# One set of 98-column products per tile in the layers' edge stage, with the values held in on-chip memory

## The reference

```python
for i in range(L):                       # L = 4
    Q = _ln(h @ Wq[i], gq[i], bq[i])
    K = _ln(h @ Wk[i], gk[i], bk[i])
    qi = Q[src]
    kj = K[dst]
    score = (qi * kj).sum(-1) + 0.1 * (edge_attr * qi[:, :RBF]).sum(-1) + logm[dst]
    smax = jax.ops.segment_max(score, src, num_segments=N)
    es = jnp.exp(jnp.minimum(score - smax[src], 20.0))
    denom = jax.ops.segment_sum(es, src, num_segments=N)
    alpha = es / (denom[src] + 1e-10)
    m = h[dst] @ Wm[i]
    aggi = jax.ops.segment_sum(alpha[:, None] * m, src, num_segments=N)
    ...
```

## Time and profile before

| | us |
|---|---|
| median of three runs | 5786.9 (5772.91 to 5797.48) |
| the profiled execution | 5777.9 |
| its span | 5776.3 |
| TensorE busy in it | 4309.7 (75%) |
| VectorE busy | 3791.9 (66%) |
| GpSimd busy | 2681.4 (46%) |
| ScalarE busy | 2250.1 (39%) |

### The profile page before, as it was taken

One profiled execution on the slowest core, in us unless ns is written; L12 is line 12 of the kernel. 1 busy time (PEld: TensorE's weight loads), 2 busy tenths in 40 slices (PEclk: granted clock), 3 DMA queues, 4 the chain that ended last, 5 costly groups with the idle time before them and its releaser, 6 DMA issues. The chain is left out here.

```text
span 5776.3 us, 186815 instructions
## 1 busy us (share of the span) xinstructions
PE 4309.7 (75%) x79576; PEld 3592.7 (62%) x79576; DVE 3791.9 (66%) x7925; ACT 2250.1 (39%) x7746; POOL 2681.4 (46%) x2702
## 2 busy tenths in 40 slices
PE   7999994046666499759976997599757845877887
PEld 4555552035555388748874887488735733877786
DVE  6888875079998588657765785687576446545244
ACT  3333331046666255435543554355401424101310
POOL 2777777756666177517751775277520510000000
PEclk7666665569998699869987998799877977988897
DMA  9322223167775344234423442344255434000000
GB/s 352 74 73 74 70 68 74 42 150 197 195 201 166 113 161 165 92 109 167 154 92 120 157 154 92 123 154 165 80 88 196 158 106 134 2 9 4 4 4 10
DMA packets 488184, 656.80 MB, mean 114 GB/s; under 512 B 316480, under 2 KB 370372, under 8 KB 484117
## 3 DMA queue, kind: packets, MB, share of 16 engines
q1 hardware_dynamic: 450965, 595.00, 32.7%
q0 software_dynamic: 33856, 48.44, 3.4%
q10 hardware_dynamic: 2496, 0.98, 0.1%
HBM read 464.16 MB, written 180.09 MB: 112 GB/s over the span
## 5 line engine op out<-in xcount | busy, mean ns | idle before, releaser
L299 POOL DMA_INDIRECT edges<-sb_bk_rec,sb_bk_pos x782 | 784.8, 1004 | 323.7 <-issue 234.0
L1688 ACT ACTIVATE sb_at_val<-banks,sb_at_prob 128x49 f32<-128x49 f32 x3800 | 776.0, 326 | 189.7 <-PE banks L1622 183.3
L1727 DVE TENSOR_REDUCE sb_at_tops<-banks 128x1 f32<-128x512 f32 x1000 | 652.5, 661 | 279.1 <-PE banks L1602 276.7
L1578 PE MATMUL banks<-sb_near,sb_at_hotT_d 128*128 128x49 bf16 x11100 | 610.3, 184 | 74.0 <-DVE sb_at_key L1709 44.5
L1536 POOL TENSOR_TENSOR sb_at_key<-sb_at_key,sb_at_attr 128x400 f32<-128x400 f32 (+1 forms) x400 | 371.8, 930 | 581.1 <-ACT sb_at_key L1672 489.9
L1580 PE MATMUL banks<-sb_queryp,sb_at_hotT_s 128*128 128x49 bf16 x11400 | 624.5, 185 | 12.8 <-issue 12.3
L1578 PEld LDWEIGHTS banks<-sb_near,sb_at_hotT_d 128*128 128x128 fp8e4 x11100 | 560.3, 96 | 79.1 <-issue 69.3
L1580 PEld LDWEIGHTS banks<-sb_queryp,sb_at_hotT_s 128*128 128x128 fp8e4 x11400 | 559.5, 96 | 15.7 <-issue 15.7
L1543 POOL TENSOR_TENSOR sb_at_val<-sb_at_val 128x490 f32<-128x490 f32 (+1 forms) x400 | 387.4, 968 | 68.9 <-ACT sb_at_val L1688 67.4
L1672 ACT COPY sb_at_key<-banks 128x490 f32<-128x490 f32 (+1 forms) x400 | 225.3, 563 | 462.9 <-PE banks L1580 460.6
L1545 POOL TENSOR_TENSOR sb_at_val<-sb_at_val 128x490 f32<-128x490 f32 (+1 forms) x400 | 386.6, 966 | 31.4
(11 more groups left out here) (692 smaller groups left out, 10166.0 us busy)
## 6 DMA issues: line engine op xcount, KB each, us to landing
sb_at_attr<-attr SPq DMA_DIRECT2D x100, 760.0 KB, 7.5
sb_at_hotT_s<-rows_src_t SPq DMA_DIRECT2D x100, 608.0 KB, 3.9
sb_at_hot_s<-rows_src SPq DMA_DIRECT2D x100, 608.0 KB, 8.6
sb_at_hotT_d<-rows_dst_t SPq DMA_DIRECT2D x100, 592.0 KB, 5.9
edges<-sb_pad SPq DMA_DIRECT2D x95, 460.0 KB, 7.0
sb_gt_rec<-edges SPq DMA_DIRECT2D x25, 1748.0 KB
sb_we_hotT<-rows_dst_t SPq DMA_DIRECT2D x52, 592.0 KB, 5.8
attr<-sb_gt_rec SPq DMA_DIRECT2D x25, 760.0 KB, 13.2
```

What stands on the lines that cost most here:

```text
L299: pool.indirect_dma_start(list1, bass.IndirectOffsetOnAxis(pos[:, t:t + 1], 0), rec[:, k, j, :], None).then_inc(sent[k], 16)
L1578: pe.matmul(ps[:, 0, H1 * j:H1 * j + H1], where, what, start=(n == 0), stop=(n == 2))
L1688: ins = act.mul(val[:, v % VB, j, 0, :], ps[:, 5, H1 * j:H1 * j + H1], prob[:, i % 2, k:k + 1])
L1727: dve.tensor_reduce(tops[:, i % 2, g:g + 1], ps[:, 3 + x % 2, 0:P * len(RG[g])], AX, ALU.max).then_inc(s_top, 1)
```

## The change

- The two sets of three 49-column products per tile, for keys (L1578) and values (L1622), become one set of three with 98 columns (`pair`, in the keys' place). A unit's result now fills half of bank 0 and half of bank 1, five tiles each.
- The query products stand apart (`ask`), in the place of `values`, in banks 2 and 5.
- ScalarE copies keys (`key`) and then values (`held`, twelve buffers) out of the banks. `pair` waits for both copies of the unit before.
- `weigh` reads `held` and stands one slot earlier; so do `remainders` and `total` (unit u − 12 instead of u − 13). The drain is one slot shorter.
- The units have 10, 10, 10 and 8 tiles instead of 10, 10, 9 and 9. `hotT_d` has two buffers, loaded after the pairs of the block two before.
- VectorE's order stays as it was, `add` included.

```diff
-    TAKE = [range(0, 10), range(10, 20), range(20, 29), range(29, KT)]
+    TAKE = [range(0, 10), range(10, 20), range(20, 30), range(30, KT)]
...
-    VB = 4
+    VB, HB = 4, 12
+    ASK = 2, 5
...
+    held = m.sb("at_held", [P, HB, 10, H1])
...
             def first(i):
                 if i >= 4:
-
-                    sp.wait_ge(s_h, Q * (i - 3))
+                    sp.wait_ge(s_mgot, i - 3)
                 sp.dma_start(flat(hotT_s, i % 4), lists["hotT_s"][i]).then_inc(s_hotT[i % 4], 16)
-                sp.dma_start(flat(hotT_d, i % 4), lists["hotT_d"][i]).then_inc(s_hotT[i % 4], 16)
+                if i >= 2:
+                    sp.wait_ge(s_pair, Q * (i - 1))
+                sp.dma_start(flat(hotT_d, i % 2), lists["hotT_d"][i]).then_inc(s_wins[i % 2], 16)
...
-            for u in range(U + LAG + 2):
+            for u in range(U + LAG + 1):
                 i, q = divmod(u, Q)
-                if 0 <= u - LAG - 2 < U:
-                    remainders(u - LAG - 2)
+                if 0 <= u - LAG - 1 < U:
+                    remainders(u - LAG - 1)
...
-            def keys(i, q):
+            def pair(i, q):
                 u = Q * i + q
...
                 if u:
                     pe.wait_ge(s_rowk, u)
-                if u >= 2:
-                    pe.wait_ge(s_dot, u - 1)
+                    pe.wait_ge(s_held, u)
+                half = len(TAKE[q]) // 2
                 for j, k in enumerate(TAKE[q]):
                     if k == NW:
                         pe.wait_ge(s_far[i % 4], 16 * (i // 4 + 1))
                     for n in range(3):
-                        where, what = place(i, k, n, 0)
-                        pe.matmul(ps[:, 0, H1 * j:H1 * j + H1], where, what, start=(n == 0), stop=(n == 2))
+                        where, what = ((hotT_d[:, i % 2, k, :], near[:, k, n, :]) if k < NW else
+                                       (c["identb"][:], far[:, i % 4, n, :]))
+                        ins = pe.matmul(ps[:, j // half, KH * (j % half):KH * (j % half) + KH], where, what, start=(n == 0),
+                                        stop=(n == 2))
+                ins.then_inc(s_pair, 1)
+
+            def ask(i, q):
+                u = Q * i + q
...
+                if u >= 2:
+                    pe.wait_ge(s_dot, u - 1)
...
-            for u in range(U + LAG + 3):
+            for u in range(U + LAG + 2):
...
-                    keys(i, q)
+                    pair(i, q)
...
-                if 0 <= u - LAG < U:
-                    values(*divmod(u - LAG, Q))
+                if i < NB:
+                    ask(i, q)
                 if laid:
                     lay(b, laid[1])
-                if 0 <= u - LAG - 3:
-                    total(*divmod(u - LAG - 3, Q))
+                if 0 <= u - LAG - 2:
+                    total(*divmod(u - LAG - 2, Q))
...
-            def key_in(u):
+            def pair_in(u):
                 n = len(TAKE[u % Q])
-                act.wait_ge(s_keys, u + 1)
+                got = ps[:, 0:2, 0:KH * n // 2].rearrange("p b (j f) -> p b j f", f=KH)
+                halves = lambda v: v[:, 0:n, :].rearrange("p (b j) f -> p b j f", b=2)
+                act.wait_ge(s_pair, u + 1)
                 if u >= 2:
                     act.wait_ge(s_score, u - 1)
-                act.copy(key[:, u % 2, 0:n, :], ps[:, 0, 0:H1 * n].rearrange("p (j f) -> p j f", f=H1)).then_inc(s_rowk, 1)
+                act.copy(halves(key[:, u % 2]), got[:, :, :, 0:H1]).then_inc(s_rowk, 1)
+                if u >= HB:
+                    act.wait_ge(s_val, u - HB + 1)
+                act.copy(halves(held[:, u % HB]), got[:, :, :, H1:KH]).then_inc(s_held, 1)
...
-                    ins = act.mul(val[:, v % VB, j, 0, :], ps[:, 5, H1 * j:H1 * j + H1], prob[:, i % 2, k:k + 1])
+                    ins = act.mul(val[:, v % VB, j, 0, :], held[:, v % HB, j, :], prob[:, i % 2, k:k + 1])
```

More of the change, by code:

```diff
@@ L1474, in attend @@
     val = m.sb("at_val", [P, VB, 10, 3, H1])
-    names = ["keys", "rowk", "key", "dot", "score", "split", "turned", "rows", "laid", "top", "max", "mgot", "shift", "prob",
-             "h", "val", "rest", "split2", "sum", "added", "link"]
+    names = ["pair", "asked", "rowk", "held", "key", "dot", "score", "split", "turned", "rows", "laid", "top", "max", "mgot", "shift",
+             "prob", "val", "rest", "split2", "sum", "added", "link"]
     rings = [f"attr{k}" for k in range(2)] + [f"hots{k}" for k in range(2)] + [f"hotT{k}" for k in range(4)] + [
-        f"far{k}" for k in range(4)] + [f"near{k}" for k in range(Q)]
+        f"wins{k}" for k in range(2)] + [f"far{k}" for k in range(4)] + [f"near{k}" for k in range(Q)]
     turned_bank = ps[:, 7, 128:192].bitcast(BF16)
     with stage(nc, "attend", *names, *rings) as (
-            block, s_keys, s_rowk, s_key, s_dot, s_score, s_split, s_turned, s_rows, s_laid, s_top, s_max, s_mgot, s_shift,
-            s_prob, s_h, s_val, s_rest, s_split2, s_sum, s_added, s_link, *dmas):
-        s_attr, s_hots, s_hotT, s_far, s_near = dmas[0:2], dmas[2:4], dmas[4:8], dmas[8:12], dmas[12:]
+            block, s_pair, s_asked, s_rowk, s_held, s_key, s_dot, s_score, s_split, s_turned, s_rows, s_laid, s_top, s_max, s_mgot,
+            s_shift, s_prob, s_val, s_rest, s_split2, s_sum, s_added, s_link, *dmas):
+        s_attr, s_hots, s_hotT, s_wins, s_far, s_near = dmas[0:2], dmas[2:4], dmas[4:8], dmas[8:10], dmas[10:14], dmas[14:]
         @block.sync
```

39 lines of the change are left out of this document (15 added, 24 removed).

## The result

| | before | after |
|---|---|---|
| median, us | 5782.3 (5772.9 to 5797.5, 4 runs) | 6004.3 (5998.3 to 6007.2, 4 runs) |
| ratio to before | | 1.038 (95% interval 1.0355 to 1.0405) |
| profiled execution's span, us | 5776.3 | 6001.8 |
| `attend`, first pair or key product to last `total`, mean of four layers | 472.1 | 528.0 |
| TensorE busy in the span | 4309.7 | 4371.3 |

The forecast was 5830 us, range 5775 to 5885. The sign was right, the size was not: +222 us instead of +43. All of it lies in `attend`: +56 us per layer, times four 224, and the spans differ by 225.5.

The account below looks back on a forecast made before the run. TensorE was taken to bound `attend`. Per layer +41.2 −18.2 −2.5 −0.5 −9.3 = +10.7 us, +43 over four layers, on the 5786.9 median gave 5830 us, range 5775 to 5885.

Parts of the forecast that it names:

- everything else: Rest of each layer: products −18.2, instruction gaps −2.5, start −0.5, drain −9.3 us; ScalarE's copies and smaller ring nothing.
- The clock: Rival, chance 5%: TensorE standing 2 of 18 us lowers its clock in `attend`, 15 to 20 us per layer, 5900 us.
- The wait: Behind `lay` 9 at the end of slot q = 0, `total` waits 1.96 us for `add`, 21 times: +41.2 us per layer.
- The products: Three 98-column products per tile, 43.5 ns each, replace six of 49 columns: −18.2 us per layer, bounds 12 and 19.
- The instruction gaps: TensorE's "issue" waits in `attend` shrink by a quarter with the number of products: −2.5 us per layer, bounds 0 and 4.
- The drain: Layer's end: 11.7 us behind the last `prob` instead of 18.6, 6.9 less; net 9.3 less per layer, bounds 6 and 12.
- ScalarE: Second copy and `weigh` from on-chip memory stay hidden behind TensorE, costing nothing; as a rival bound, 5920 us, chance 3%.
- the ring: `hotT_d` with two buffers instead of four: its load still lands well ahead of use, costing nothing.
- the start: First slots of a layer, to slot 10: 0.5 us earlier per layer, bounds −1 and +3.

Follow-up runs that it names:

- last run: Kernel after, with `add` moved to the head of VectorE's slot q = 0 and the divide's third operation between the last two `top`s: 5640.7 us, ratio to before 0.975.
- middle-add run: Kernel after, with VectorE's `add` moved between the last `top`s and `largest` of slot q = 0: ratio to before 0.9954.
- run 1769: Not a run label: 1769 or 1770 is the count of products between TensorE's "issue" stops in the last run.
- the run with the late total: Kernel after, with TensorE's `total` put back to thirteen slots behind the keys: 5888.7 us, ratio to before 0.9765.
- one small fill: Kernel after, with the unit's query products repeated once (0.77 us) ahead of `total` in slots q = 0 from the fifth block on: 6203.3 us, ratio to before 1.0289.
- filled with 2.3 of work: Kernel after, with the unit's query products repeated three times ahead of `total` in slots q = 0 from the fifth block on: ratio to before 1.0145.

## Why the prediction was wrong

The last run has the whole change and, in mid-stage, no wait for VectorE and full clock; so it divides the 56 us per layer. Without the waits the change gives 472.1 − 435.6 = 36 us back. The kernel after is 92 above that. Of these, 89 lie between the first `maxima` and the last query product of a layer: the 21 waits of `total` for the `add` there are 54, the remaining 35 are the clock. The other 3 lie behind the last query product. Two more waits for the `add` stand there (5.2 and 2.3 us in the first layer, in the page's 61.6), but most of their time is not lost by them: in the last run TensorE stands there too, for `turn_scores` and `maxima`. The middle-add run checks the division: between the same two points it is 34 us above the last run, and its waits there add up to 33.

| per layer, us | forecast | measured |
|---|---|---|
| wait of `total` for the `add`, 21 times | +41.2 | +54 |
| clock | 0 (a rival, 5%) | +35 |
| everything else | −30.5 | −33 |
| sum | +10.7 | +56 |

*The clock: the step that failed.* The sum put it at nothing, and it cost 35 us per layer. The prediction named it as a rival, priced it at a twentieth of the stage at half clock and gave it 5%. The granted clock of 0.90 in mid-stage is a fifth of the time at half. (The price was wrong in itself as well: a twentieth of 450 us at half clock can cost no more than 11 us, not 15 to 20. The share, too small by four, is the larger error.) What it gave as the reason against it, "the stretches here stay at about 86%", looked at the mean busy share; the middle-add run has TensorE busy 91% and the kernel after 87%, and their clocks are 1.00 and 0.90. The rows of before could not have priced this: they hold no wait of 2 us that comes back in each block. But the bound should have been drawn from the other side: a lost clock makes the products behind the wait twice as long, and with the slot that follows it slow in each of 21 blocks (about 2 us each) that is an estimated 40 us per layer, more than the wide products were to bring. With the 35 that were measured, the sum would be 10.7 + 35 = 46 us per layer, 5970.

*The wait: right in place and number, mis-sized.* It is where the prediction put it, behind the last laid-out group, with the chain of the earlier trace rows, and it comes 21 times per layer ahead of the drain. In two to five of the 21 blocks it is 1.9 us, as forecast, in the others 2.7. Its length was read from a block of the kernel before in which the divide's three operations took 0.20 each, with GpSimd idle from 2206.76 to 2207.71. The block was no odd one: the third operation takes 0.20 in all 20 of that stretch (mean 199 ns), so more blocks of before would have said the same. "VectorE has 20% to spare, so it isn't later than here" was the wrong argument: its load did not change, but what GpSimd does beside it did, since the attributes are now added when the third operation starts. The row that gave warning stood in the same trace: `shifted`'s second operation, equally small, took 0.80 us there (mean 767 ns in 2040 to 2400 us), beside a GpSimd operation. From the same view of before, VectorE by form:

```profile
L1746 DVE TENSOR_TENSOR sb_at_shift<-sb_at_shift,sb_at_sparts 128x38 f32<-128x38 f32 x21 | 16.1, 767 | 0.7
```

With those lengths the 21 waits are 54 us instead of 41. The missing 45 us per layer of the forecast are thus the clock (35) and the mis-sized wait (13), less 3 that the rest brought beyond its forecast.

*The products: right in kind, a little too good.* 98-column products start 46 ns apart, in a stream 45.1 on average. Forecast 43.5, bounds 43 and 47. From starts, pairs take 5.14 us per block where keys and values took 5.77: 0.63 saved instead of 0.81, about 14 us per layer instead of 18.2. By the Trainium skill's rule in "TensorE: Matmul & The Clock Gate", section "Back-to-back issue gap", an estimate of 62 ns in proportion, they would have cost more than they saved. The traces have 46, and every run without the wait in mid-stage is faster than before.

*The instruction gaps: far too small.* In mid-stage of before, the distances of over 0.3 us between two of TensorE's starts add up to 0.75 us per block; in the last run four are left in 340 us, 0.15 us per block, and most of its blocks take 15.9 us. That is some 13 us per layer where the forecast took a quarter of the "issue" waits, 2.5. (Products 14 and stops 13 are 27; the middle of a layer became 24 shorter, its start, end and drain the other 12 of the 36.) What these stops were, the traces don't say; they name "issue". They do lie at fixed distances in TensorE's own program: in the kernel before 507 or 508 products apart, or 380, or 888, the sum of both; in the last run 1769 or 1770. So they can't be scaled by the number of products, as the forecast did.

*The drain: nearly right, for another reason.* 12.3 us behind the last `prob`, forecast 11.7, before 18.6; so 6.3 saved of 6.9. I had expected 4 to 9 us per layer to go with the earlier total; the run with the late total shows that it is nothing. And what sets those 12.3 us is not GpSimd's remainders, as the prediction had it, but ScalarE's 38 weighings in a row, 2.3 us for ten, the distance at which the last `total`s follow each other (timeline of the kernel after, its drain):

```profile
2486.06 8.70 ACT L1692 ACTIVATE sb_at_val<-sb_at_held,sb_at_prob 128x49 f32<-128x49 f32 x38
```

*ScalarE, the ring, the start: nothing or next to it, as said.* Ten weighings from `held` (ScalarE's timeline, in mid-stage):

```profile
2236.27 2.37 ACT L1692 ACTIVATE sb_at_val<-sb_at_held,sb_at_prob 128x49 f32<-128x49 f32 x10
```

They start 0.227 us apart against 0.185 from the banks, some 42 ns more, and not the 27 of the earlier trace rows. The estimate of 43 ns from the Trainium skill ("VectorE: DVE Perf Modes", section "The TRN2 errata — SBUF-src ops pay a fixed extra latency per instruction") agrees with that. ScalarE has 243 us of 300 busy in the fastest version and still holds nothing up in mid-stage.

## What to carry to other kernels

Ahead of an edit that puts a wait into the bounding TensorE stream once per block, price the clock behind it as well: here waits of 1.9 to 2.7 us in each block cost some 60% of themselves again (23 us on 40, 35 on 54), and waits of 1.6 us only themselves. Where such a wait can't be avoided, try work that is thrown away in its place: here it gave back 2.2%. When an operation is pulled forward, look at where its consumer stands in every other engine's program, and move that too: one line of VectorE's order decided between 4% slower and 2% faster.

## What the runs showed of the hardware

- TensorE's granted clock against one recurring wait, all in the same stage: 1.6 us per block of 17.7, 1.00; 1.9 to 2.0 with one small fill, 0.94; 1.9 in the kernel before, 0.91; 2.1, 0.91; 2.6 to 2.7, 0.89 and 0.90; 2.7 filled with 2.3 of work, 1.00.
- A VectorE operation of 128x38 with both inputs on chip takes 0.20 us when it starts alone. When it starts while a GpSimd two-input operation is running it ends 0.05 to 0.06 us behind that one, in all 51 such cases of the kernel after from 2040 to 2400 us, and so takes 0.35 to 1.03. VectorE's larger operations with one input in the banks (L1714, 0.66 us) took the same beside GpSimd.
- Products of 49 columns start 25.3 ns apart, of 98 columns 46 ns; at half clock most of 98 columns start 81 to 85 ns apart.
- TensorE's "issue" stops of 0.4 to 2.3 us recur at fixed counts of products (507 or 508, 380, 888 in the kernel before; 1769 or 1770 in the last run).
- Ten ScalarE multiplications of 128x49 overlap: 0.185 us between starts with the source in the banks, 0.227 with the source in on-chip memory.
